# Scores ahead of the transposes in a fused cross attention and mixture-of-experts kernel, with keys stored apart and read in 64-float runs

## The chip, the cores and the metric

The kernel runs on one core of a Trainium2 chip. The time is that of the device for one execution, in microseconds; the lower the better. Three executions of the kernel before were timed, and one was profiled.

## What is computed

128 independent batches of 128 tokens with 256 channels go through an attention block and a feed-forward block. Attention is across the 16 heads of one token, not across tokens: for each token a 16 x 16 matrix of scores. Cut to what matters:

```python
q = (layernorm(x) @ Wq.T).reshape(B, N, H, D)      # H = D = 16
k = (ctx @ Wk.T).reshape(B, N, H, D)
v = (ctx @ Wv.T).reshape(B, N, H, D)
attn = softmax(einsum('bnhd,bngd->bnhg', q, k) * SCALE, axis=-1)
x = x + transpose(einsum('bnhg,bngd->bnhd', attn, v), (0, 2, 1, 3)).reshape(B, N, C) @ Wp.T + bp
n = layernorm(x)
shared = (silu(n @ sfc1.T) * (n @ sfc2.T)) @ sfc3.T
top_w, top_idx = top_k(n @ gate_w.T, 2); top_w = softmax(top_w)
moe = sum over the two chosen experts e of top_w * (silu(n @ w1[e].T) @ w2[e].T)
out = x + moe + shared
```

## The kernel before

The work has two stages. In the first a loop goes over 32 chunks of four batches (512 tokens, four tiles of 128). Body c of the loop mixes three chunks: the attention of chunk c, the shared feed-forward and the routing of chunk c-1, and the projections of chunk c+1. The routed rows are scattered to lists in DRAM. In the second stage the lists are read back by expert, four tiles at a time, and go through the experts' matrices; the change does not touch it.

Every engine has its own program, written out by hand in the order in which it runs, and waits on counting semaphores. For the change these parts matter:

- **TensorE**, body c: `scores(c)` (128 matmuls, L1202, of blocks of q, `q_rows`, with blocks of keys, `k_diag`) into the banks A0 and A1; `gate(c-1)` (L1211) from the transposed rows `xn2_t` (printed as th) into A2; `project(c+1)`: four tiles of keys and values in the banks U, A0, Y0, Y1 (L1187 to L1189, three matmuls for each half of the channels, since operands are split in a high and a low part), then two pairs of q tiles in A1 and U; then the shared feed-forward of c-1 in steps z and u, with `attend(c)` (L1345) and `attend_out(c)` (L1361, L1366) in between; `shared_down(c-1)` (48 matmuls into Y0 and Y1, out of wsh_out and hid_hi, hid_lo); last `turn(c)`, eight transposes (L1387) of the normalised rows xn into Z0 and Z1.
- **ScalarE**, body c: the exponentials of the probabilities (L564) and of the routing (L598, needs VectorE's routing, which needs the gate); `project_out(c+1)`: four copies of keys and values from PSUM (L582), one store of 1 MB (L584), four scaled copies of q (L590), a store of 512 KB (L593); then `load_res(c)`, the load of the residual rows (L633, behind a wait on base_ready); tanh and rounding of the shared part; the normalisation (L647, four instructions); `turned_out(c)`: two copies of the transposed rows to th (L653), rounding of the next x (L573), rounding of th (L658).
- **SP**, chunk c: loads of the next x and ctx, then, when the scores of c-1 are done, eight reads of keys (L277), eight of q (L282), and, when the attention of c-1 is done, eight of values (L290). They turn the layout round: from token on the partition, as stored, to head channel (keys, q) or head (values) on the partition. All 24 read 64 KB each in runs of 16 floats, 1024 runs each.
- **GpSimd**, body c: the low parts of th (xn_lo), base scatters (L421), half of the scaling of the probabilities (L450), eight slot scatters (L412) and four low parts of the hidden rows (L443, hid_lo) by turns; small powers; then the low parts of ctx and x for c+2 (L426, ctx_lo and hid_lo). `shared_down` waits for three of the four hid_lo at its start and for the fourth after 18 matmuls.
- **VectorE**, body c: row maxima (L790) and shift (L784) of the scores, routing, sums, transposes of the probabilities, products of the shared part, `bias_add(c)` on the residual rows (L922), attention's low parts (L917), the residual sums (L931, which count h2_ready) and moments.

`w_sb` stands for several tensors in the printed names, among them `w2_sb`, which holds the keys and values on their way to DRAM and `q_rows`. hid_hi and hid_lo hold x's parts too.

## Time and profile before

| | us |
|---|---|
| three timed runs | 1759.50, 1761.28, 1775.06 |
| median | 1761.28 |
| profiled execution, as timed | 1761.56 |
| its span in the profile | 1759.7 |

| engine | busy us | share | instructions |
|---|---|---|---|
| PE (TensorE matmul) | 1510.9 | 86% | 17237 |
| PEld (TensorE weight load) | 1321.4 | 75% | 17238 |
| DVE (VectorE) | 1279.3 | 73% | 3352 |
| ACT (ScalarE) | 747.6 | 42% | 1442 |
| POOL (GpSimd) | 1308.6 | 74% | 1252 |

How to read the rows further down. A row of the timeline has the start in us, the duration, the engine, the line of the kernel, the operation, what it writes and reads, shapes, the number of instructions merged in it, and in brackets the engine's idle time before it with what ended it. SPq and ACTq are the queues' issues of DMAs; such a row's duration is the time in which they were issued, not the transfer. A row of the waits has: engine and line, what it waited for, us in total, times, the longest in us. A row of sums by window has: the window, its length, then for PE, PEld, DVE, ACT and POOL the busy us with the number of instructions in brackets, then the granted clock of TensorE as a share of full speed (2.4 GHz; 0.5 is the lower level of 1.2 GHz), the busy share of the DMA engines, and GB/s. Starts and ends of matmuls overlap, since they are pipelined.

### The profile page before, as it was taken

Reading aid. Unit: us, or ns where it says so; the run is one execution under the profiler, and the core shown is the slowest. Engines: PE = TensorE matmul, PEld = TensorE weight load, DVE = VectorE, ACT = ScalarE, POOL = GpSimd, SP = SyncE. Lnnn points to the kernel's source line nnn. Section 1 sums busy time; section 2 is a strip of 40 time slices with the busy share of each in tenths; the row PEclk is TensorE's granted clock in tenths of the full one; section 3 lists DMA queues with packets and bytes.
Section 4 is the critical chain, followed back from the end, with each engine's and each line's share of the span. In section 5 each row is a group of like instructions: output and inputs, shape, how many; then the busy total and the mean of one; then the engine's idle time right before and its main releaser. Section 6 shows DMA issues by size and latency. Waiting matters only on the chain.

```text
span 1759.7 us, 50976 instructions
## 1 busy us (share of the span) xinstructions
PE 1510.9 (86%) x17237; PEld 1321.4 (75%) x17238; DVE 1279.3 (73%) x3352; ACT 747.6 (42%) x1442; POOL 1308.6 (74%) x1252
## 2 busy tenths in 40 slices
PE   5599999999999999999999999987577677777774
PEld 4488888888888888888888888875577676676764
DVE  7578888788888878887888886886455655555553
ACT  3344455444554455454554454533133333332331
POOL 4277787777788777887787877776587777677776
PEclk9799999999999999999999999998798988888987
DMA  8788888888888887898888888873778777677773
GB/s 221 125 198 194 178 176 188 209 188 185 165 207 207 179 176 165 225 195 172 175 172 236 182 180 164 179 189 116 243 232 241 232 236 220 178 234 229 225 222 109
DMA packets 945836, 340.80 MB, mean 194 GB/s; under 512 B 824571, under 2 KB 899213, under 8 KB 940771
## 3 DMA queue, kind: packets, MB, share of 16 engines
q1 hardware_dynamic: 892464, 166.19, 53.3%
q0 software_dynamic: 33600, 88.95, 13.6%
q10 hardware_dynamic: 19728, 85.13, 12.8%
q8 instruction: 21, 0.34, 0.1%
q14 instruction: 23, 0.18, 0.0%
HBM read 200.37 MB, written 148.15 MB: 198 GB/s over the span
## 4 chain that ended last, share of the span: by engine, by line
SPq 26%; issue 22%; PE 17%; DMA 12%; POOL 8%; DVE 7%; another core or an unknown queue 4%; ACT 3%; DVEq 1%; POOLq 0%; ACTq 0%
SPq L277 10%; SPq L282 9%; DMA kv_dram<-w_sb 5%; SPq L290 5%; DMA w_sb<-q_dram 4%; POOL sums L529 3%; PE bank_a L1202 3%; POOL out L529 2%; PE bank_y L1187 2%; POOL xn_lo L521 2%; PE bank_y L1189 2%; DMA h<-in_x_res 2%; PE bank_y L1188 2%; PE bank_z L1473 2%
## 5 line engine op out<-in xcount | busy, mean ns | idle before, releaser
L412 POOL DMA_INDIRECT slots<-xn,slot_i x256 | 277.5, 1084 | 86.0 <-issue 71.4
L1142 DVE SCALAR_TENSOR_TENSOR v_area<-bank_y,tail,v_area 128x256 f32<-128x256 f32 x288 | 121.9, 478 | 129.9 <-PE bank_y L1189 65.5
L1187 PE MATMUL bank_y<-w_hi,xn_hi 128*128 x288 | 100.7, 350 | 110.7 <-POOL xn_lo L521 94.5
L529 POOL DMA_INDIRECT out<-v_area,tail x144 | 147.1, 1021 | 57.2 <-issue 34.4
L529 POOL DMA_INDIRECT sums<-v_area,tail x144 | 147.9, 1027 | 43.8 <-issue 35.9
L729 ACT ACTIVATE th<-bank_z 128x512 f32<-128x512 f32 x72 | 43.0, 598 | 285.1 <-PE bank_z L1473 151.1
L1187 PEld LDWEIGHTS bank_y<-w_hi,xn_hi 128*128 128x128 f32 x288 | 60.0, 208 | 128.4 <-issue 128.1
L421 POOL DMA_INDIRECT sums<-k_area,slot_i x128 | 126.7, 990 | 35.8 <-issue 30.1
L1187 PE MATMUL bank_y<-wsh_out_hi,hid_hi 128*128 128x256 f32 x512 | 142.1, 278 | 0.0
L1189 PE MATMUL bank_y<-wsh_out_hi,hid_lo 128*128 128x256 f32 x512 | 142.1, 278 | 0.0
L1188 PE MATMUL bank_y<-wsh_out_lo,hid_hi 128*128 128x256 f32 x512 | 142.0, 277 | 0.0
L614 ACT ACTIVATE th<-bank_z 128x512 f32<-128x512 f32 x128 | 76.2, 596 | 114.9 <-PE bank_z L1189 56.4
L1120 DVE SCALAR_TENSOR_TENSOR v_area<-th,bank_z 128x512 f32<-128x512 f32 x72 | 49.3, 684 | 96.9 <-ACT th L729 48.9
L790 DVE TENSOR_REDUCE row_max<-bank_a 128x32 f32<-128x512 f32 x64 | 44.3, 692 | 91.8 <-PE bank_a L1202 91.8
L647 ACT ACTIVATE xn<-h,ln_shift,ln_rstd 128x256 f32<-128x256 f32 x128 | 66.6, 592 | 101.2 <-POOL ln_shift L402 98.2
L619 ACT ACTIVATE hid_hi<-k_area 128x512 fp32r<-128x512 f32 x64 | 40.5, 632 | 162.6 <-DVE k_area L900 102.9
L1187 PE MATMUL bank_z<-xn_hi,w_lo 128*128 128x512 f32 x256 | 105.0, 410 | 5.0 <-DVE th L890 2.7
L443 POOL TENSOR_TENSOR hid_lo<-k_area,hid_hi 128x512 fp32r<-128x512 f32 x64 | 83.0, 1296 | 28.0 <-ACT hid_hi L619 27.2
L1189 PE MATMUL bank_z<-xn_hi,w_lo 128*128 128x512 f32 x256 | 101.7, 397 | 0.0
L1188 PE MATMUL bank_z<-xn_lo,w_lo 128*128 128x512 f32 x256 | 101.2, 395 | 0.0
L1473 PE MATMUL bank_z<-k_area,x_sb 128*128 128x128 f32 x576 | 89.3, 320 | 12.3 <-ACT k_area L722 11.0
L722 ACT ACTIVATE k_area<-bank_a 128x512 f32<-128x512 f32 x144 | 80.6, 597 | 45.0 <-issue 19.9
(234 smaller groups left out, 5314.2 us busy)
## 6 DMA issues: line engine op xcount, KB each, us to landing
k_area<-slots SPq DMA_DIRECT2D x288, 129.0 KB
v_area<-sums SPq DMA_DIRECT2D x288, 128.0 KB
kv_dram<-w_sb ACTq DMA_DIRECT2D x32, 1024.0 KB
x_sb<-in_x_in SPq DMA_DIRECT2D x32, 512.0 KB
ctx_sb<-in_ctx_t SPq DMA_DIRECT2D x32, 512.0 KB
q_dram<-q_sb ACTq DMA_DIRECT2D x32, 512.0 KB
k_area<-kv_dram SPq DMA_DIRECT2D x256, 64.0 KB
w_sb<-q_dram SPq DMA_DIRECT2D x256, 64.0 KB
```

The source lines that it names most:

```text
L277: sp.dma_start(k_diag[rows, :, t % 4, :], kv[src, :, :, 0, :].rearrange("n i (d g) -> d (n i) g", d=D)).then_inc(S["qk_read"], 16)
L282: sp.dma_start(q_rows[rows, :, t // 4 * H:(t // 4 + 1) * H], q[src].rearrange("n i (d h) -> d (n i) h", d=D)).then_inc(S["qk_read"], 16)
L290: sp.dma_start(v_diag[16 * r:16 * r + 16, :, r % 4, :], kv_t2[t2, :, i, 1, :].rearrange("m (g d) -> g m d", g=H)).then_inc(S["v_read"], 16)
L412: pool.indirect_dma_start(slots[j], bass.IndirectOffsetOnAxis(ap=slot_i[:, par, j, i:i + 1], axis=0), row_of[j][:, i, :], None).then_inc(S ...
L421: pool.indirect_dma_start(sums[FIRST], bass.IndirectOffsetOnAxis(ap=slot_i[:, par, FIRST, i:i + 1], axis=0), base[:, i, :], None).then_inc ...
L443: nc.gpsimd.tensor_tensor(hid_lo[:, s, :], hid_of[s], hid_hi[:, s, :], ALU.subtract).then_inc(S["hid_split"], 1)
L529: pool.indirect_dma_start(target, bass.IndirectOffsetOnAxis(ap=tail[:, r, t, 1 - j:2 - j].bitcast(u32), axis=0), y_ring[:, r, t, :], None, ...
L1142: st = nc.vector.scalar_tensor_tensor(out=y_ring[:, r, t, :], in0=Y[t // 2][:, t % 2 * C:(t % 2 + 1) * C], scalar=tail[:, r, t, j:j + 1], ...
L1187: mm(out, lhs_hi, rhs_hi, start=start, stop=False)
L1188: mm(out, lhs_hi, rhs_lo, start=False, stop=False)
L1189: return mm(out, lhs_lo, rhs_hi, start=False, stop=stop)
L1473: last = mm(Z[r % 2][:, t * P:(t + 1) * P], w1_slot[r % 2][:, t, k * HID:(k + 1) * HID], x_ring_t[:, t, k * P:(k + 1) * P], start=k == 0, ...
```

## The change

Three things are changed in the chunk loop.

- Keys and values go to DRAM apart, `k_dram` and `v_dram`, by two stores of 512 KB: keys, then q, then values. ScalarE's copy writes the keys in the order channel of the head, tile, head, so that for one channel the 16 heads of all four tiles are 64 floats in a row, and `k_diag` takes them in that order. A key read has 256 runs of 64 floats. Reads of q and of values keep 16 floats.
- TensorE computes `scores(c)` ahead of `turn(c-1)`, with a wait for the residual sums of c-1, whose banks the scores take, and `gate(c-1)` stands behind the first tile of keys and values of `project(c+1)`.
- ScalarE issues the load of the residual ahead of `project_out`.

```diff
-                kv = kv_dram[c].rearrange("(t n) (i w f) -> t n i w f", t=8, i=BPC, w=2)
+                k = k_dram[c].rearrange("(t n) (d i g) -> t d n (i g)", t=8, d=D, i=BPC)
...
-                    sp.dma_start(k_diag[rows, :, t % 4, :],
-                                 kv[src, :, :, 0, :].rearrange("n i (d g) -> d (n i) g", d=D)).then_inc(S["qk_read"], 16)
+                    sp.dma_start(k_diag[rows, :, t % 4, :, :].rearrange("p n i g -> p n (i g)"), k[src]).then_inc(S["qk_read"], 16)
...
-                    nc.scalar.activation(kv_sb[:, i, :], KV_BANKS[i][:, :], ACT.Copy).then_inc(S["kv_out"], 1)
+                    nc.scalar.activation(kv_by_tile[:, i], KV_BANKS[i][:, :].rearrange("p (w x y) -> p w x y", w=2, x=D), ACT.Copy).then_inc(S["kv_out"], 1)
                 act.wait_ge(S["kv_out"], at(4, c, 4))
-                act.dma_start(kv_dram[c], kv_sb).then_inc(S["kv_stored"], 16)
+                act.dma_start(k_dram[c], k_sb).then_inc(S["k_stored"], 16)
...
                 act.dma_start(q_dram[c], q_sb[:, :, :]).then_inc(S["q_stored"], 16)
+                act.dma_start(v_dram[c], v_sb).then_inc(S["v_stored"], 16)
...
-                if ahead:
-                    project_out(c + 1, False)
                 if first:
                     act.wait_ge(S["w_ffn_split"], 2)
                 else:
                     act.wait_ge(S["base_ready"], at(2, c - 1, 0))
                 load_res(c, par)
+                if ahead:
+                    project_out(c + 1, False)
...
                 pe.wait_ge(S["qk_read"], at(256, c, 256))
+                if not first:
+                    pe.wait_ge(S["h2_ready"], at(2, c, 0))
...
                             last = mm(SCORE_BANKS[u][32 * a:32 * a + 32, n * 4 * H:(n + 1) * 4 * H], q_rows[:, m, :],
-                                      k_diag[:, m, :, :].rearrange("p t g -> p (t g)"), start=True, stop=True)
+                                      k_diag[:, u * 8 + n, :, QUARTER_OF[a], :], start=True, stop=True)
...
                     last.then_inc(S["kv_full"], 1)
+                    if gate_of is not None and i == 0:
+                        gate(gate_of)
...
             def body(c, first, ahead):
                 scores(c, False)
-                gate(c - 1)
+                turn(c - 1)
                 if ahead:
-                    project(c + 1, False, True, first)
+                    project(c + 1, False, True, first, c - 1)
+                else:
+                    gate(c - 1)
...
                 shared_down(c - 1, first)
-                turn(c)
```

On TensorE, at the start of body 1, before (ident and xn are the transposes, k_area with w_sb the scores, wgate_sb the gate, w_hi with ctx_hi the keys and values):

```order
L1387 MATMUL bank_z<-ident,xn 128x128 [waits const_ready,xn2_ready,const_in,w_ffn]
L1387 MATMUL bank_z<-ident,xn 128x128 [waits xn2_ready] x3
L1387 MATMUL bank_z<-ident,xn 128x128 x4
L1202 MATMUL bank_a<-k_area,w_sb 32x64 [waits qk_read]
L1202 MATMUL bank_a<-k_area,w_sb 32x64 x63
L1211 MATMUL bank_a<-th,wgate_sb 32x128 [waits t2_out]
L1211 MATMUL bank_a<-th,wgate_sb 32x128 x7
L1187 MATMUL bank_u<-w_hi,ctx_hi 128x512 [waits ctx_split]
L1188 MATMUL bank_u<-w_hi,ctx_hi 128x512
L1189 MATMUL bank_u<-w_hi,ctx_lo 128x512
```

And there after the change (lines are those of the changed kernel):

```order
L1209 MATMUL bank_a<-k_area,w_sb 32x64 [waits qk_read,const_ready,h2_ready,const_in,w_ffn]
L1209 MATMUL bank_a<-k_area,w_sb 32x64 x63
L1396 MATMUL bank_z<-ident,xn 128x128 [waits xn2_ready] x4
L1396 MATMUL bank_z<-ident,xn 128x128 x4
L1192 MATMUL bank_u<-w_hi,ctx_hi 128x512 [waits ctx_split]
L1193 MATMUL bank_u<-w_hi,ctx_hi 128x512
L1194 MATMUL bank_u<-w_hi,ctx_lo 128x512
L1192 MATMUL bank_u<-w_hi,ctx_hi 128x512
L1193 MATMUL bank_u<-w_hi,ctx_hi 128x512
L1194 MATMUL bank_u<-w_hi,ctx_lo 128x512
L1218 MATMUL bank_a<-th,wgate_sb 32x128 [waits t2_out]
L1218 MATMUL bank_a<-th,wgate_sb 32x128 x7
```

The scores moved from behind the transposes to ahead of them, with the wait for h2_ready, and the gate from ahead of the first tile in bank U to behind it.

On ScalarE, in a body behind the loop that still projects ahead, before:

```order
L598 ACTIVATE gap_e<-top 128x1 x3
L582 ACTIVATE w_sb<-bank_u 128x512 [waits kv_full,q_stored,kv_stored]
L582 ACTIVATE w_sb<-bank_a 128x512 [waits kv_full]
L582 ACTIVATE w_sb<-bank_y 128x512 [waits kv_full] x2
L584 DMA kv_dram<-w_sb 128x2048 [waits kv_out]
L590 ACTIVATE q_sb<-bank_a,ln_rstd 128x256 [waits q_full,ln1_pow]
L590 ACTIVATE q_sb<-bank_a,ln_rstd 128x256
L590 ACTIVATE q_sb<-bank_u,ln_rstd 128x256 [waits q_full]
L590 ACTIVATE q_sb<-bank_u,ln_rstd 128x256
L593 DMA q_dram<-q_sb 128x1024 [waits q_out]
L633 DMA h<-in_x_res 128x1024 [waits base_ready]
```

And after:

```order
L603 ACTIVATE gap_e<-top 128x1 x3
L638 DMA h<-in_x_res 128x1024 [waits base_ready]
L586 ACTIVATE w_sb<-bank_u 128x32x16 [waits q_stored,kv_full,v_stored,k_stored]
L586 ACTIVATE w_sb<-bank_a 128x32x16 [waits kv_full]
L586 ACTIVATE w_sb<-bank_y 128x32x16 [waits kv_full] x2
L588 DMA k_dram<-w_sb 128x1024 [waits kv_out]
L594 ACTIVATE q_sb<-bank_a,ln_rstd 128x256 [waits q_full,ln1_pow]
L594 ACTIVATE q_sb<-bank_a,ln_rstd 128x256
L594 ACTIVATE q_sb<-bank_u,ln_rstd 128x256 [waits q_full]
L594 ACTIVATE q_sb<-bank_u,ln_rstd 128x256
L597 DMA q_dram<-q_sb 128x1024 [waits q_out]
L598 DMA v_dram<-w_sb 128x1024
```

The residual's load moved from the end to the head of these rows, the one store became two, and the values' store stands behind q's.

## Rows read from the trace of the kernel before

**Rows 1.** Sums by window: the middle of the loop, and 804 to 808 us.
```profile
400.00:800.00 400.00, 387.04 (x5058) 332.12 (x5057) 337.89 (x875) 200.47 (x397) 317.36 (x278) 1.00 0.86 189
804.00:808.00 4.00, 3.69 (x140) 3.69 (x144) 0.76 (x2) 1.49 (x3) 3.47 (x2) 0.57 0.58 57
```
**Rows 2.** Instructions of line 790, 150 to 1170 us: min/median/max ns, first and last start.
```profile
L790 DVE TENSOR_REDUCE row_max<-bank_a x58: 691/692/693, 154.4 to 1169.4; 128x32 f32<-128x512 f32 x58
```
**Rows 3.** Timeline of PE, the head of the chunk at 547.5 us.
```profile
547.52 0.54 PE L1387 MATMUL bank_z<-ident,xn 128*128 128x128 f32 x2
...
548.71 0.77 PE L1387 MATMUL bank_z<-ident,xn 128*128 128x128 f32 x5 [0.16 <-ACT xn L647]
549.67 1.99 PE L1202 MATMUL bank_a<-k_area,w_sb 128*32 128x64 f32 x128 [0.20 <-DMA w_sb<-q_dram]
551.49 0.66 PE L1211 MATMUL bank_a<-th,wgate_sb 128*32 128x128 f32 x16
552.07 0.50 PE L1187 MATMUL bank_u<-w_hi,ctx_hi 128*128 128x512 f32 x1
```
**Rows 4.** Waits, 150 to 1170 us.
```profile
DVE h L922 <- DMA h<-in_x_res: 20.6, 22, 2.2
PEld bank_a L1202 <- DMA w_sb<-q_dram: 14.7, 18, 2.9
```
**Rows 5.** Timeline of PE, the scores of the three longest waits.
```profile
333.38 3.60 PE L1202 MATMUL bank_a<-k_area,w_sb 128*32 128x64 f32 x128 [1.17 <-DMA w_sb<-q_dram]
...
804.31 3.57 PE L1202 MATMUL bank_a<-k_area,w_sb 128*32 128x64 f32 x128 [1.57 <-DMA w_sb<-q_dram]
...
1058.56 3.64 PE L1202 MATMUL bank_a<-k_area,w_sb 128*32 128x64 f32 x128 [2.66 <-DMA w_sb<-q_dram]
```
**Rows 6.** Timeline of SP's queue, the chunk behind the one of rows 3.
```profile
555.26 0.51 SPq L263 DMA_DIRECT2D x_sb<-in_x_in  x1
...
565.69 7.53 SPq L277 DMA_DIRECT2D k_area<-kv_dram  x8
573.40 7.89 SPq L282 DMA_DIRECT2D w_sb<-q_dram  x8
```
**Rows 7.** Timeline of PE: first matmul of the down projection, first transposes behind it.
```profile
578.04 0.28 PE L1187 MATMUL bank_y<-wsh_out_hi,hid_hi 128*128 128x256 f32 x1
...
583.49 0.53 PE L1387 MATMUL bank_z<-ident,xn 128*128 128x128 f32 x2
```
**Rows 8.** Timeline of POOL, from the context's low part to the last hidden part.
```profile
548.10 2.36 POOL L426 TENSOR_TENSOR ctx_lo<-ctx_sb,ctx_hi 128x1024 fp32r<-128x1024 f32 x1
551.27 2.39 POOL L426 TENSOR_TENSOR hid_lo<-hid,hid_hi 128x1024 fp32r<-128x1024 f32 x1 [0.81 <-ACT hid_hi L573]
...
576.60 0.96 POOL L412 DMA_INDIRECT slots<-xn,slot_i  x1 [0.30 <-issue]
578.20 1.30 POOL L443 TENSOR_TENSOR hid_lo<-k_area,hid_hi 128x512 fp32r<-128x512 f32 x1 [0.64 <-ACT hid_hi L619]
```
**Rows 9.** Timeline of ACT, the copies of the transposed rows.
```profile
549.07 1.08 ACT L653 ACTIVATE th<-bank_z 128x512 f32<-128x512 f32 x2 [0.42 <-PE bank_z L1387]
```
**Rows 10.** Timeline: bias addition in two chunks; first transposes behind the second.
```profile
534.07 1.23 DVE L922 TENSOR_TENSOR h<-h,bias_sb 128x1024 f32<-128x1024 f32 x1 [1.36 <-DMA h<-in_x_res]
...
605.54 2.96 DVE L922 TENSOR_TENSOR h<-h,bias_sb 128x1024 f32<-128x1024 f32 x1 [1.32 <-DMA h<-in_x_res]
...
620.41 0.53 PE L1387 MATMUL bank_z<-ident,xn 128*128 128x128 f32 x2
```
**Rows 11.** Timeline of SP's queue and of PE in the first 80 us.
```profile
27.54 5.54 SPq L277 DMA_DIRECT2D k_area<-kv_dram  x8
...
59.44 3.64 PE L1345 MATMUL bank_a<-v_area,w_sb 128*32 128x64 f32 x128 [10.29 <-DMA v_area<-kv_dram]
...
72.48 2.71 PE L1387 MATMUL bank_z<-ident,xn 128*128 128x128 f32 x8 [4.90 <-ACT xn L647]
...
76.47 3.64 PE L1202 MATMUL bank_a<-k_area,w_sb 128*32 128x64 f32 x128 [1.28 <-DMA w_sb<-q_dram]
```

## What the change will do to the time

> **What bounds the kernel now.** I read the sums by window first. Between 400 and 800 us, in the middle of the chunk loop, TensorE is busy 387 of 400 us at the full clock, VectorE 338, GpSimd 317 [rows 1]. The loop is bound by TensorE, and there is little idle time to win. The row maxima of the scores, two a chunk, run from 154.4 to 1169.4 us in 58 instances [rows 2]: 28 chunks and some 0.9 us, so a chunk takes (1015 - 0.9) / 28 = 36.2 us. The expert stage behind the loop is not touched by the change, and I leave it as it is.
>
> The busy share hides short waits, so next I read the timeline of TensorE around the head of one ordinary chunk [rows 3]. I call D the moment at which the down projection has issued its last matmul, here 547.52. The transposes (L1387) start at once but come in pieces, two, one and five, because each waits for ScalarE's normalised rows. Scores (L1202) start at 549.67 after 0.20 us of waiting for q's rows to land, the gate (L1211) at 551.49, the first tile of keys and values at 552.07, D + 4.55. The scores themselves need 1.82 us, the gate 0.58, eight transposes without waits about 8 x 0.11 = 0.9 (five take 0.77 with the 0.33 tail of one). That is 3.3 of the 4.55 us; the rest is the wait for the rows and for the DMA.
>
> Then who else is nearly late. The waits of the stretch say that the scores waited for q's rows 18 times in 29 chunks, 14.7 us by the weight loads, and that VectorE's bias addition (L922) waited 20.6 us 22 times for the residual's load [rows 4]. The longest of the first kind cost more than the wait: in three chunks TensorE idled 1.17, 1.57 and 2.66 us, and the 128 score matmuls that followed took 3.60, 3.57 and 3.64 us in place of 1.99 [rows 5]. The stretch at 804 us was granted 0.57 of the clock, mostly the 1.2 GHz level, where the loop else has 1.00 [rows 1]: after a longer pause the engine ran at the lower level.
>
> **The change, step by step.** *Layout of the keys.* A key read moves the same 64 KB in 256 runs of 64 floats, not 1024 of 16. Eight reads keep SP for 7.53 us, the eight of q for 7.89 behind them, until 581.29, 2.2 us ahead of this chunk's end at D = 583.49 [rows 6, 7]; landing takes about that, since the scores of the chunk before waited 0.20 us for q's rows and started at D + 2.15 [rows 3]. Nothing in this trace has 256-byte runs of this kind. If only bytes counted, eight reads would stay at 7.5 us, if only runs counted 1.9. I take 4.0, nearer to the runs, since the stores and loads with long runs hold their queues for far less per byte (an input of 512 KB takes SP 0.51 us, all eight key reads together move that much) [rows 6]. So q's rows land about 3.5 us sooner, near D - 1.4. For the new order to work they must come at least 2.15 us sooner, so 1.35 us are to spare. The Trainium skill, DMA: Bandwidth & Descriptors, section "Why small descriptors are slow (HBM only)", gives a fixed 3 cycles a packet beside one per 32 bytes: 5 cycles for 64 bytes, 11 for 256. By that estimate eight reads would take 7.53 x 11 / (4 x 5) = 4.1 us; no run here shows it yet.
>
> *Two stores.* 512 KB of keys go first, then q, then the values. Bytes are unchanged, keys can only be readable sooner. I count nothing for it: the values are read by a queue that reaches them after key and q reads, after 7.53 and 7.89 us of other reads [rows 6], and ScalarE's one more issue (SP's of an input takes 0.51) falls where it waits for TensorE anyway. The copies of keys and values write 16-float pieces, and the scores read them with a stride; ScalarE's and TensorE's durations should not change, and if the copies took half as long again, four of them would be 1.2 us a chunk on an engine that is busy 200 of 400 us [rows 1].
>
> *Order on TensorE.* From D: scores 1.82; the rows are normalised by then, so the transposes run through, 0.9, to D + 2.7. The first tile of keys needs GpSimd's low part of the context, which ends at 548.10 + 2.36 = D + 2.94 [rows 8]: start at D + 3.0. The gate behind it costs its 0.58. The second tile therefore stands where it would stand with a first tile at D + 3.58: 4.55 - 3.58 = 0.97 us sooner. The added wait for the residual sums is over by then (they precede the normalised rows). The second tile's bank waits for VectorE's shifted scores; they have the transposes, the first tile and the gate as cover, where before they had the gate and the tile. The gate ends at D + 5.0, before at D + 4.55. Behind it wait VectorE's routing, then ScalarE's four gap exponentials, and behind those on ScalarE the key and value copies (L582) and so kv_out, which TensorE needs for attention and shared banks; ScalarE comes to them only after the probabilities' exponentials, which the transposes' copies move back anyway.
>
> *What is late next.* ScalarE's copies of the transposed rows (L653) start at 549.07, D + 1.55 [rows 9]; with the scores ahead they start at D + 1.82 + 0.44 + 0.3 = D + 2.56, one microsecond later, and all that follows them: the rounding of x, then GpSimd's hid_lo at 551.27 [rows 8]. From there GpSimd has a long fixed list (two splits, four base scatters, the scaling of the probabilities, eight slot scatters, three hidden splits) until 576.60 + 0.96 = 577.56, that is 26.29 us. Then comes the fourth hidden split, which in this chunk waited 0.64 us for ScalarE and took 1.30 [rows 8]. TensorE asks for it 18 matmuls (two tiles, three quarters, three each) after the start of the down projection, whose 48 take 583.49 - 578.04 = 5.45 us: 578.04 + 18 x 0.1135 = D + 32.56 [rows 7]. Before: done at 579.50, D + 31.98, in time. After: D + 4.75 + 26.29 + 0.15 + 1.30 = D + 32.49, wanted at D + 31.59. GpSimd would be 0.9 us late, and give back nearly all of the 0.97. So a chunk gains between 0.06 us (the list as long as here) and 0.97 (the list never late). The list holds instructions stretched by other engines (below), and in other chunks is shorter; I take 0.4.
>
> *The residual's load* is issued ahead of ScalarE's eight copies and the stores, not behind them. That ends L922's waits [rows 4]. Such a wait cost a chunk time where it pushed the addition into GpSimd's scatters: 1.23 us at 534.07, but 2.96 at 605.54 after 1.32 us of waiting, and that chunk lasted from 583.49 to 620.41, 36.9 us, against 36.0 for the one before [rows 7, 10]. I credit 0.1 us a chunk.
>
> *Start.* The first chunks are a chain of reads on SP: key reads of 5.54 us from 27.54, then TensorE waits 10.29 us for the values until 59.44, then 4.90 for normalised rows, then 1.28 for q's rows, and the scores run 3.64 us at the low clock [rows 11]. Shorter key reads bring all this forward by about 2 us, and the second set of them lets scores stand inside the 4.90 us wait: 1.28 + 3.64. Together 7 us, between 4 (half of the second part) and 10.
>
> **Sum.** 28 chunks x 0.5 = 14.0; the three long chunks lose their excess, (1.17 - 0.20) + (3.60 - 1.99) = 2.6, then 3.0 and 4.1, 9.7 together; start 7. That is 30.7 us of the profiled span, 1759.7 to 1729. The median of the runs, 1761.28, lies 1.6 above that span (the profiled execution itself was timed at 1761.56), so the time is 1731 us.
>
> **The rivals.** *TensorE keeps everything* (20%). GpSimd's list turns out shorter by 0.9 us, because fewer of its instructions meet VectorE's. For it: its busy share is 317 of 400. Then 28 x 0.97 = 27, with 9.7 and 10: 1714.
>
> *GpSimd takes the loop* (17%). The list stays at 26.3 us, a chunk gains under 0.1: 1761.3 - 9.7 - 7 - 1.7 = 1743. For it: the list above, worked out for a chunk of ordinary length.
>
> *Reads still late* (6%). Eight key reads keep more than 5.3 us, or q's store is not there. Scores then wait with the transposes behind them, first tile at D + 2.1 + 1.82 + 0.9 = 4.8: no gain in a chunk, the long ones stay; 4 us of the start: 1757.
>
> *Slower, through the port of VectorE and GpSimd* (8%). The bias addition no longer waits and GpSimd is 1 us later, so the two meet at another place. If the addition takes 2.96 us in every chunk, each lasts 36.9 in place of 36.2: 28 x 0.7 = 20 us more, less the 7 of the start: 1774. It decides once a mean chunk is 0.25 us longer than now. Against it: most chunks meet somewhere already. The Trainium skill, SBUF — State Buffer, section "SBUF: two separate sides", says that a VectorE operation with two SBUF inputs and a GpSimd operation that reads SBUF exclude each other for a whole instruction; the two durations of L922 agree with that.
>
> The remaining 4% are for what I don't see. My own case (45%) has 1722 to 1742.
>
> **Chances.** About 1% is what a measurement of this kernel can tell from no change: 17.6 us, a limit of 1743.7. Faster by more: my case, the first rival and half of the second, 0.73. Slower by more (over 1779) only with a part of the last: 0.04. The range goes from the first rival's 1714, a little widened, to what is left when GpSimd takes the loop and the long chunks stay: 1761 - 7 - 2 = 1752.
>
> **What would show it.** Right: scores directly behind the down projection with no wait for q's rows, transposes in one piece, key reads at about 4 us for eight, no stretch of low clock in the loop, L922 without waits, and new waits of the down projection (L1187, bank_y) for GpSimd's hid_lo of up to 0.9 us. A chunk near 35.4 us with these. Wrong: no such waits and a chunk of 34.9; key reads near 7 us; or the waits of the down projection above 1 us. The expert stage has to take the same time.

## The result, and the profile after

Over twenty runs of each kernel on one chip the changed kernel takes 1754.6 us (median, 1745.19 to 1768.6), the kernel before 1766.92 us (1757.25 to 1776.45). The ratio is 0.9934, with a 95% interval of 0.9913 to 0.9955: faster by two thirds of a percent, which is inside the 1% that I called no change. I had forecast 1731 us, a ratio of 0.983 to the 1761.28 us known then, and a range of 1712 to 1752 us. The result lies outside that range on the slow side. Part of this is the kernel before, which took 5.6 us more over twenty runs than over the three known then; the ratio times 1761.28 is 1749.7 us, just inside the range. The profiled execution has a span of 1752.3 us, against 1759.7 before.

The first view is the same as in [rows 1] and [rows 2]: busy time by window and the row maxima of the scores (L795, L790 before), for the changed kernel. The last row is that of the kernel before, with one more chunk at its start than in [rows 2].

```profile
400.00:800.00 400.00, 387.11 (x5052) 331.50 (x5045) 310.07 (x876) 200.82 (x407) 321.32 (x277) 1.00 0.82 189
804.00:808.00 4.00, 4.00 (x22) 3.38 (x21) 3.41 (x6) 0.97 (x3) 3.25 (x4) 1.00 0.63 190
L795 DVE TENSOR_REDUCE row_max<-bank_a x60: 690/692/693, 108.4 to 1152.7; 128x32 f32<-128x512 f32 x60
```
```profile
L790 DVE TENSOR_REDUCE row_max<-bank_a x60: 691/692/693, 114.8 to 1169.4; 128x32 f32<-128x512 f32 x60
```

TensorE is as busy as before. The maxima of the third chunk come 6.4 us sooner (108.4 against 114.8), those of the last 16.7 us sooner: 6.4 us were won at the start and 10.3 in 29 chunks. A chunk takes (1152.7 - 108.4 - 0.9) / 29 = 35.98 us, against 36.33 worked out in the same way, where I expected 35.4. The sum credited the three long chunks with 9.7 us, and they are gone; so the ordinary chunks won 0.6 us together (10.3 less 9.7), where the sum had 14. Measured from D to D, the chunks with the full clock took 35.92 us in the mean before (24 of 27) and take 36.01 us now (27 of 27). The span shrank by only 7.4 us; the other 9.3 went in the expert stage, which the change doesn't touch. The profiled executions of this study differ by tens of microseconds there, so I compare chunks by profiles and whole kernels by ratios.

The head of a chunk, attention and the chunk's neighbours, in the changed kernel. Timelines: start, duration, engine, line; in brackets the idle time ahead and what ended it.

```profile
575.50 1.99 PE L1209 MATMUL bank_a<-k_area,w_sb 128*32 128x64 f32 x128
577.42 1.09 PE L1396 MATMUL bank_z<-ident,xn 128*128 128x128 f32 x8
578.44 0.50 PE L1192 MATMUL bank_u<-w_hi,ctx_hi 128*128 128x512 f32 x1
...
596.43 0.65 PE L1354 MATMUL bank_a<-v_area,w_sb 128*32 128x64 f32 x31
597.43 1.27 PE L1354 MATMUL bank_a<-v_area,w_sb 128*32 128x64 f32 x66 [0.36 <-issue]
599.17 0.33 PE L1354 MATMUL bank_a<-v_area,w_sb 128*32 128x64 f32 x3 [0.47 <-issue]
599.89 0.67 PE L1354 MATMUL bank_a<-v_area,w_sb 128*32 128x64 f32 x28 [0.40 <-issue]
600.49 0.50 PE L1192 MATMUL bank_z<-xn_hi,w_lo 128*128 128x512 f32 x1
```
```profile
580.31 2.41 POOL L429 TENSOR_TENSOR hid_lo<-hid,hid_hi 128x1024 fp32r<-128x1024 f32 x1 [1.93 <-ACT hid_hi L576]
...
595.36 1.54 POOL L415 DMA_INDIRECT slots<-xn,slot_i  x1 [0.30 <-issue]
596.93 1.28 POOL L446 TENSOR_TENSOR hid_lo<-hid,hid_hi 128x512 fp32r<-128x512 f32 x1
598.38 0.99 POOL L415 DMA_INDIRECT slots<-xn,slot_i  x1 [0.17 <-issue]
...
606.39 1.30 POOL L446 TENSOR_TENSOR hid_lo<-k_area,hid_hi 128x512 fp32r<-128x512 f32 x1 [0.55 <-ACT hid_hi L624]
```
```profile
588.63 4.85 SPq L279 DMA_DIRECT2D k_area<-k_dram  x8
...
594.85 1.22 DVE L927 TENSOR_TENSOR h<-h,bias_sb 128x1024 f32<-128x1024 f32 x1
```

The head is what I had drawn: with D, the end of the down projection's issue as in the prediction, at 575.41, scores at D + 0.09 with no wait, eight transposes in one piece, the first tile of keys at D + 3.03. L927 (L922 before) no longer waits, and no stretch of the loop runs at the low clock. What I hadn't drawn is the attention, the 128 matmul rows of L1354: from 596.43 to 600.49 they take 4.06 us and stop three times, for 0.36, 0.47 and 0.40 us, with no semaphore behind it ("issue"). The waits of the loop say how often. First the changed kernel, 150 to 1170 us, then the kernel before, 150 to 1150 us: engine, tile, line, what was waited for; us in total, times, longest.

```profile
PEld bank_a L1354 <- issue: 54.4, 113, 1.3
PE bank_a L1354 <- issue: 30.4, 84, 0.5
```
```profile
PEld bank_a L1345 <- issue: 20.3, 55, 0.7
PE bank_a L1345 <- issue: 5.3, 20, 0.5
```

So what the head won was gone before the chunk's end: the median attention grew from 2.4 to 3.8 us (first matmul of it to the next section's first). Where it doesn't stop it takes 1.9. The question for the experiments was what stops it, and whether that sets the chunk's length.

### The profile page after: what moved, and what is told of

Its sections match the earlier page's. It is cut to its first block, busy times and chain, and to the rows that moved or that the text cites. A ratio compares the mean times of both kernels' runs of the same rounds, so it can differ in the third digit from the quotient of the medians.

```text
span 1752.3 us, 50714 instructions
## 1 busy us (share of the span) xinstructions
PE 1506.9 (86%) x17237; PEld 1323.2 (76%) x17238; DVE 1214.8 (69%) x3352; ACT 740.1 (42%) x1442; POOL 1310.0 (75%) x1252
## 3 DMA queue, kind: packets, MB, share of 16 engines
q1 hardware_dynamic: 695856, 166.19, 48.9%
## 4 chain that ended last, share of the span: by engine, by line
PE 65%; issue 15%; POOL 6%; another core or an unknown queue 5%; DVE 3%; SPq 3%; ACT 1%; DMA 1%; DVEq 0%; POOLq 0%; ACTq 0%
PE bank_y L1194 7%; PE bank_y L1192 7%; PE bank_y L1193 7%; PE bank_a L1354 5%; PE bank_z L1192 4%; PE bank_a L1209 3%; PE bank_z L1194 3%; PE bank_z L1193 3%; PE bank_a L1192 3%; POOL out L532 3%; PE bank_u L1192 3%; PE bank_u L1194 2%; PE bank_u L1193 2%; PE bank_a L1194 2%
## 5 line engine op out<-in xcount | busy, mean ns | idle before, releaser
L429 POOL TENSOR_TENSOR hid_lo<-hid,hid_hi 128x1024 fp32r<-128x1024 f32 x32 | 78.1, 2439 | 65.0 <-ACT hid_hi L576 65.0
L1354 PE MATMUL bank_a<-v_area,w_sb 128*32 128x64 f32 x4096 | 90.2, 223 | 41.8 <-issue 30.8
L1354 PEld LDWEIGHTS bank_a<-v_area,w_sb 128*32 128x32 f32 x4096 | 70.7, 111 | 67.6 <-issue 56.4
L1483 PE MATMUL bank_z<-k_area,ctx_sb 128*128 128x128 f32 x576 | 91.9, 326 | 31.5 <-ACT k_area L727 28.7
L895 DVE SCALAR_TENSOR_TENSOR th<-th,bank_z 128x512 f32<-128x512 f32 x128 | 87.5, 683 | 36.7 <-issue 30.6
L1483 PEld LDWEIGHTS bank_z<-k_area,ctx_sb 128*128 128x128 f32 x576 | 86.7, 238 | 34.6 <-ACT k_area L727 25.1
L1192 PE MATMUL bank_z<-xn_hi,w_lo 128*128 128x512 f32 x256 | 105.1, 410 | 5.5 <-POOL xn_lo L429 2.8
L812 DVE STREAM_TRANSPOSE w_sb<-w_sb 64x512 f32<-64x512 f32 x128 | 90.4, 706 | 17.3 <-POOL w_sb L453 14.1
```

Of the source, the lines that this page charges most:

```text
L429: nc.gpsimd.tensor_tensor(lo, value[:, :, :], hi, ALU.subtract).then_inc(S[done], 1)
L812: nc.vector.transpose(turned_half(u, f), prob[rows, u, :].rearrange("p (s h) -> p s h", h=H)).then_inc(S["p_ready"], 1)
L895: nc.vector.scalar_tensor_tensor(out=th[:, s % 2, :], in0=th[:, s % 2, :], scalar=1.0, in1=Z[s % 2][:, :], op0=ALU.add, op1=ALU.mult).then ...
L1192: mm(out, lhs_hi, rhs_hi, start=start, stop=False)
L1354: last = mm(O_BANKS[u][32 * pair:32 * pair + 32, n * 4 * D:(n + 1) * 4 * D], prob_t[:, 32 * g:32 * g + 32], v_diag[:, pair * 16 + u * 8 + ...
L1483: last = mm(Z[r % 2][:, t * P:(t + 1) * P], w1_slot[r % 2][:, t, k * HID:(k + 1) * HID], x_ring_t[:, t, k * P:(k + 1) * P], start=k == 0, ...
```

## The experiments

Eighteen runs were made in five sets, of thirteen edited kernels (e1 to e13) and five repeats (c1 to c5); those that share a chip and a median of the kernel before in the table were timed beside the same runs of it. The letters stand for four chips; whether the first chip is one of them isn't on record. On chip B the kernel before itself moved from 1776.41 to 1755.99 us between two sets, so ratios are compared inside a set, and what compares chips is weaker. "Attention" is the median of the loop's chunks, measured as above; a chunk is worked out from the row maxima, as for the result.

| run | chip | kernel before, us | ratio [95%] | chunk, us | attention, us |
|---|---|---|---|---|---|
| result | first | 1766.92 | 0.9934 [0.9913, 0.9955] | 36.0 | 3.8 |
| e1, PE loop written out | A | 1776.5 | 0.9999 [0.9974, 1.0023] | 36.1 | 3.8 |
| e2, V store later | A | 1776.5 | 1.0016 [0.9990, 1.0043] | 36.1 | 3.9 |
| e3, delay at the head | A | 1776.5 | 1.0186 [1.0165, 1.0206] | 36.9 | 3.9 |
| e4, code shifted | A | 1776.5 | 1.0008 [0.9984, 1.0031] | 36.0 | 3.9 |
| c1, changed again | B | 1776.41 | 0.9985 [0.9965, 1.0006] | 36.0 | 3.9 |
| e5, scatters off the attention | B | 1776.41 | 1.0008 [0.9984, 1.0032] | 35.8 | 1.9 |
| e6, no q reads | B | 1776.41 | 1.0012 [0.9988, 1.0036] | 35.8 | 3.8 |
| e7, layout only | B | 1776.41 | 0.9876 [0.9830, 0.9922] | 35.3 | 2.5 |
| e8, x rounded first | B | 1755.99 | 0.9792 [0.9740, 0.9844] | 34.9 | 2.4 |
| e9, e8 and last scatter late | B | 1755.99 | 1.0059 [1.0033, 1.0085] | 36.1 | 1.9 |
| e10, e7 and last scatter late | B | 1755.99 | 1.0526 [1.0460, 1.0591] | 38.7 | 1.9 |
| e11, order only | B | 1755.99 | 1.0243 [1.0179, 1.0307] | 37.3 | 3.7 |
| e12, e8 and five scatters first | C | 1698.38 | 1.0266 [1.0241, 1.0291] | 37.2 | 1.9 |
| e13, residual load only | C | 1698.38 | 0.9986 [0.9970, 1.0003] | 35.6 | 1.9 |
| c2, e8 again | C | 1698.38 | 0.9862 [0.9840, 0.9885] | 34.9 | 1.95 |
| c3, changed a third time | D | 1708.14 | 0.9813 [0.9787, 0.9838] | 35.0 | 1.94 |
| c4, layout only again | D | 1708.14 | 0.9853 [0.9826, 0.9880] | 35.2 | 1.97 |
| c5, e8 a third time | D | 1708.14 | 0.9802 [0.9777, 0.9827] | 34.9 | 1.95 |

### Set 1: is it the code, the traffic, or the supply?

e1 replaces TensorE's loop by straight code:

```diff
-            with pe.Fori(2, CHUNKS - 1) as c:
+            for c in range(2, CHUNKS - 1):
                 body(c, False, True)
```

> The changed kernel with TensorE's loop over chunks 2 to 30 written out 29 times, nothing else. In the changed kernel the attention matmuls (128 rows of 32x64) take 3.8 us in a loop chunk, with pauses of 0.6 us in which no semaphore is waited for, and 1.8 us in the chunks 1 and 31 that stand outside the loop. Theory L (the pauses belong to the hardware loop: its jump, or where its body lies in memory): the attention takes 1.8 to 2.0 us in every chunk, a chunk 34 to 35 us, the whole 1715 to 1730 us. Theory D (the transfers in flight at that moment hold TensorE's instructions up): nothing changes, attention 3.8 us, the whole within 5 us of the changed kernel's 1754.6. Theory S (TensorE's sequencer can supply only so many instructions per chunk, whatever the code looks like): nothing changes either.

e2 issues the store of V later on ScalarE:

```diff
                 act.dma_start(q_dram[c], q_sb[:, :, :]).then_inc(S["q_stored"], 16)
-                act.dma_start(v_dram[c], v_sb).then_inc(S["v_stored"], 16)
...
                 o_round(sums_of)
+                act.dma_start(v_dram[c + 2], v_sb).then_inc(S["v_stored"], 16)
```

> The changed kernel, but the store of V (1 MB less a half: 128x1024 floats) leaves ScalarE's queue only after the attention output has been rounded, some 5 us after the attention matmuls, so that it isn't in flight beside them. Theory D (transfers in flight hold up TensorE's instructions): the attention drops from 3.8 us towards 1.9 to 2.4 us and a chunk from 36.0 towards 35 us, the whole towards 1725 us. Theories L and S: attention stays at 3.8 us, the whole within 5 us of 1754.6; it may get longer where V's reads come late.

e3 and e4 add matmuls, the one in every chunk, the other once, ahead of everything:

```diff
                 scores(c, False)
+                for i in range(4):
+                    mm(KV_BANKS[0][:, :], wsh_hi[:, 0, 0:P], wsh_hi[:, 0, 0:BANK], start=True, stop=True)
                 turn(c - 1)
```

> The changed kernel with four extra f32r matmuls of 128x512 (about 0.23 us each, 0.9 us together) between the scores and the transposes of every chunk but the first. Their result is overwritten. Theory S (the supply of instructions sets the pace; what TensorE saves at the head it waits in the attention): the attention gets shorter by nearly the same 0.9 us, a chunk stays within 0.2 us of 35.99, the whole within 6 us of 1754.6. Theories L and D: attention stays at 3.8 us, a chunk takes 0.9 us more, the whole is 1780 us.

```diff
                     pe.wait_ge(S["ones_ready"], 1)
+                    for i in range(32):
+                        mm(WQ_SUM_BANK[0:32, 0:64], ones_f[:, 0:32], ones_f[:, 0:64], start=True, stop=True)
```

> The changed kernel with 32 extra small fp32 matmuls (32x64) in TensorE's program ahead of the first projection, where TensorE waits for its weights anyway (under 2 us once, hidden or not). Inside the loop every instruction is the same, but stands further on in memory. Theory L in the form that the place of the body in memory decides where the supply pauses: the pauses of 0.6 us move to another place of the chunk (by about 64 to 128 rows), and the attention's 3.8 us change; a chunk may take 34.5 to 36.5 us. Theories D and S, and L in the form that the jump itself costs the time: the pauses stay at the attention's rows 28 to 31 and 107 to 125, the whole within 5 us of 1754.6.

None of the four moved the attention by more than 0.1 us. (The changed kernel itself was not run on chip A; the four are held against it by chunk and attention, not by ratio.) e1 is the cleanest, since the DMA view counts the fetched code; its row for queue q8 (packets, MB, share), which rises with TensorE's written-out program, in the changed kernel and in e1:

```profile
q8 instruction: 21, 0.34, 0.1%
```
```profile
q8 instruction: 122, 2.00, 0.5%
```

With the loop written out 101 more blocks are fetched, and the pauses are the same, the first most often after 29 or 30 of the 128 matmuls in both kernels: neither the jump nor the fetching of code makes them. e4 added 32 matmuls ahead of the loop and left the pauses in place (the first after 27 to 30 in 23 of 28 chunks). e3's added 1.04 us came out as 0.9 us more a chunk with the attention unchanged, so TensorE is not held by a fixed supply per chunk either. e2 left the first pause and brought the second forward, from 2.74 to 2.29 us behind the attention's start in the median, and GpSimd's second scatter issue of that stretch moved alike, from 2.14 to 1.68. That was the hint: the pauses keep their distance to GpSimd's indirect DMA issues, not to TensorE's own code.

### Set 2: GpSimd's scatters, q's reads, and the change in parts

> The changed kernel as it is, run beside the others so that they are compared on one chip. Every theory: 0.993 of the kernel before, attention 3.8 us in a loop chunk, a chunk 36.0 us.

```diff
-                scatter(c - 1, 1 - par, SCATTERS[:4])
-                hid_split(c - 1, range(1))
-                scatter(c - 1, 1 - par, SCATTERS[4:5])
-                hid_split(c - 1, range(1, 2))
-                scatter(c - 1, 1 - par, SCATTERS[5:6])
+                scatter(c - 1, 1 - par, SCATTERS[:3])
+                hid_split(c - 1, range(2))
+                scatter(c - 1, 1 - par, SCATTERS[3:5])
                 hid_split(c - 1, range(2, 3))
-                scatter(c - 1, 1 - par, SCATTERS[6:])
+                scatter(c - 1, 1 - par, SCATTERS[5:])
```

> The changed kernel with GpSimd's list in another order: three slot scatters, both first hid_lo subtractions, two scatters, the third subtraction, three scatters, the last subtraction (as it is: four scatters, subtraction, scatter, subtraction, scatter, subtraction, two scatters, subtraction). Same instructions, but none of GpSimd's indirect DMA issues (1.0 to 1.7 us each; in the changed kernel one from 1.0 us ahead of the attention to 0.7 us into it, the next from 2.15 to 3.1 us into it) falls into the attention matmuls. Theory P (while GpSimd issues an indirect DMA, TensorE's sequencer gets its instructions late, which shows only where TensorE runs its shortest instructions): attention falls from 3.8 to 1.9 to 2.2 us, a chunk from 36.0 to 34.2 to 34.8 us, the whole by 35 to 50 us against the changed kernel of this call. Theory Q (the reads of q's rows in 64-byte pieces, in flight through the attention, hold it up): attention stays at 3.5 to 3.9 us, the whole within 5 us.

In e6 SP's loop over the eight reads of q runs in the first chunk alone, and TensorE waits for 128 instead of 256 a chunk.

> The changed kernel without the eight reads of q's rows from the second chunk on: scores are made from the rows of chunk 0, so their values aren't the reference's; every matmul and everything else still runs. Theory Q (these reads hold TensorE up in the attention): attention 1.9 to 2.2 us, a chunk 34.5 us. Theory P (GpSimd's indirect DMA issues do): attention stays at 3.4 to 3.9 us and a chunk within 0.4 us of 36.0; the pauses keep their place beside GpSimd's issues.

e7 takes the changed kernel and puts TensorE's body back:

```diff
                 scores(c, False)
-                turn(c - 1)
+                gate(c - 1)
                 if ahead:
-                    project(c + 1, False, True, first, c - 1)
+                    project(c + 1, False, True, first)
...
                 shared_down(c - 1, first)
+                turn(c)
```

> The changed kernel with TensorE's order of before (transposes at the end of the chunk, gate behind the scores), so only the layout of keys, the two stores and the residual load's new place are left of the change. By my prediction's sum the layout alone should give nothing in an ordinary chunk (the head is 6.45 us either way) and take away the long chunks and some of the start: 0.990 to 0.997 of before. Theory P: the attention matmuls stand where they stood against GpSimd's list, so they take 2.2 to 2.8 us, not 3.8, and the kernel is as fast as the changed one or faster: the order's gain is what the pauses take back. Theory Q: the reads of q's rows again overlap the attention by their earlier start, so attention is 3 us or more.

e6 fells theory Q: with no q reads in flight the attention still takes 3.8 us. e5 agrees with theory P. Its attention and GpSimd beside it:

```profile
630.61 2.21 PE L1352 MATMUL bank_a<-v_area,w_sb 128*32 128x64 f32 x128
```
```profile
628.42 0.96 POOL L415 DMA_INDIRECT slots<-xn,slot_i  x1 [0.30 <-issue]
629.41 1.30 POOL L446 TENSOR_TENSOR hid_lo<-hid,hid_hi 128x512 fp32r<-128x512 f32 x1
631.59 1.36 POOL L446 TENSOR_TENSOR hid_lo<-hid,hid_hi 128x512 fp32r<-128x512 f32 x1 [0.88 <-ACT hid_hi L622]
633.11 0.98 POOL L415 DMA_INDIRECT slots<-xn,slot_i  x1 [0.16 <-issue]
```

One piece, 1.92 us up to the next section (the row's 2.21 holds the tail of the last matmul), with a subtraction of GpSimd beside it and no issue: what goes with the pauses is the indirect DMA issue, not GpSimd's work as such. The reverse stands in e10 (below), inside one kernel: in 8 of its 26 attentions between 150 and 1150 us two issues fall into the attention, which takes 3.75 to 4.47 us; in the other 18 none does, and it takes 1.92 to 1.94. One of the eight:

```profile
674.07 1.76 PE L1351 MATMUL bank_a<-v_area,w_sb 128*32 128x64 f32 x108
675.98 0.27 PE L1351 MATMUL bank_a<-v_area,w_sb 128*32 128x64 f32 x3 [0.15 <-issue]
676.70 0.32 PE L1351 MATMUL bank_a<-v_area,w_sb 128*32 128x64 f32 x4 [0.44 <-issue]
677.45 0.32 PE L1351 MATMUL bank_a<-v_area,w_sb 128*32 128x64 f32 x4 [0.44 <-issue]
```
```profile
675.42 0.99 POOL L415 DMA_INDIRECT slots<-xn,slot_i  x1 [0.15 <-issue]
676.71 0.96 POOL L415 DMA_INDIRECT slots<-xn,slot_i  x1 [0.30 <-issue]
```

But the second half of my expectation failed: a chunk of e5 takes 35.8 us, not 34.2 to 34.8. The down projection (48 matmuls, 5.53 us without waits) now takes 6.39, since hid_lo(3), GpSimd's fourth and last low part of the hidden rows, ends at D + 32.2. Part of that is e5's own order: the second subtraction, at 631.59, now waits 0.88 us for ScalarE. So e5 shows that the pauses go with the issues, and not what a chunk would take without pauses and with the list as it was. e7 was a surprise the other way: the layout without the order, expected at 0.990 to 0.997, is 0.988, a chunk of 35.3 us, with its attention at 2.5 us as theory P had it.

### Set 3: GpSimd's start

In the changed kernel ScalarE rounds x behind the copies of the transposed rows, and these now come later. e8 turns the two around:

```diff
             def turned_out(c, ahead_2, early=False):
+                if ahead_2 and early:
+                    act.wait_ge(S["acc_full"], at(2, c - 1, 2))
+                    x_round(c + 2)
                 for k in range(KT):
                     act.wait_ge(S["t2_full"], at(KT, c, k + 1))
                     nc.scalar.activation(xn2_t[:, k, :], XN2T_BANKS[k][:, :], ACT.Copy).then_inc(S["t2_out"], 1)
-                if ahead_2:
+                if ahead_2 and not early:
                     x_round(c + 2)
```

> The changed kernel with one step of ScalarE moved: the rounding of x for the chunk after next (x_hi) stands ahead of the copies of the transposed rows instead of behind them, behind a wait for the down projection. In the changed kernel these copies wait for the transposes, which now come 2.0 us later in the chunk, so x_hi is ready 4.83 us after the down projection (D) instead of 3.68, and GpSimd's x subtraction starts at D+4.91 instead of D+3.76; its list then runs to hid_lo(3) at D+32.2, nearly without a stop. Theory G (the loop of the changed kernel is held by GpSimd's list, which starts 1.15 us later: any pause in the attention that goes away only comes back as a wait for hid_lo(3), as the quiet order showed: attention 1.92 us, down projection 6.39 instead of 5.53, chunk 35.7): here the subtraction starts at about D+3.0, so a chunk falls to what TensorE takes with pauses, 34.5 to 35.5 us, the whole to 0.97 to 0.988 of before. Without theory G (TensorE's pauses alone set the changed kernel's 35.99): a chunk within 0.3 us of 36.0.

e9 and e10 add to e8 and to e7 one order of GpSimd's list: scatters [:4], two subtractions, [4:6], the third, [6:7], the fourth, [7:]. e11 is the kernel before with TensorE's new body alone.

> As the run before it, and GpSimd's list in an order that keeps its indirect DMA issues out of the attention matmuls: four scatters, two hid_lo subtractions, two scatters, the third subtraction, a scatter, the fourth subtraction, the last scatter. If both halves hold (GpSimd's list starts early enough, and its issues cause TensorE's pauses): attention 1.9 us, no wait for hid_lo(3) (down projection 5.5 us), a chunk 33.9 to 34.5 us, the whole 0.96 to 0.975 of before. If only GpSimd's start mattered: the same as the run before it.

> The layout-only kernel (TensorE's order of before; 0.988 of before, a chunk 35.1 us, attention 2.5 us) with the same order of GpSimd's list as in the run before it. Theory P: attention 1.92 us in every loop chunk, a chunk 34.4 to 34.8 us, unless GpSimd's wait for hid_hi(1) makes its list too late (then down projection over 5.6 us and a chunk 35 us); the whole 0.97 to 0.985 of before.

> The kernel before with only TensorE's new order (scores, transposes, keys of tile 0, gate, the rest); layout, stores and the place of the residual load as before. By my prediction's sum the order alone wins 0.97 us at the head less 0.5 given back: a chunk 35.9 us. Theory G: GpSimd's x subtraction starts at D+4.9 here too and the chunk is bound at 35.7 to 36.0 us; the reads of keys and queries, still in pieces of 64 bytes, must be done 1.9 us earlier against D than before, so the scores wait for them in most chunks: a chunk 36 to 36.6 us, the whole 1.00 to 1.01 of before.

e8 is the fastest version: 0.979 of before. Its timeline, with D at 594.61:

```profile
594.70 1.99 PE L1212 MATMUL bank_a<-k_area,w_sb 128*32 128x64 f32 x128
...
615.66 2.43 PE L1357 MATMUL bank_a<-v_area,w_sb 128*32 128x64 f32 x128
```
```profile
597.52 2.41 POOL L429 TENSOR_TENSOR hid_lo<-hid,hid_hi 128x1024 fp32r<-128x1024 f32 x1
...
615.63 1.79 POOL L415 DMA_INDIRECT slots<-xn,slot_i  x1 [0.16 <-issue]
...
624.55 1.29 POOL L446 TENSOR_TENSOR hid_lo<-k_area,hid_hi 128x512 fp32r<-128x512 f32 x1 [0.64 <-ACT hid_hi L624]
```

The subtraction of x (hid_lo, 128x1024) starts at D + 2.91 instead of D + 4.90, and hid_lo(3) at the end of the list waits for ScalarE and no one waits for it. The list's earlier start also moved it against the attention, where now one issue falls instead of two, and 2.37 us are left. So e8 changes two things at once, the list's end and the pauses; set 5 says more on which of them counts.

e9 kept the attention at 1.92 us, e10 in 18 chunks of 26, and both lost more elsewhere. The waits of e9, 150 to 1100 us (e10 has 126.6 us in 25 chunks on the same row):

```profile
ACT xn L651 <- DMA slots<-xn,slot_i: 142.2, 26, 6.1
```

A scatter reads the rows of xn2 that ScalarE overwrites next. Behind the last subtraction it lands so late that normalisation ends at D + 3.5 (e9) where it ended at D + 1.14. In e10, where the scores stand behind the transposes, TensorE waits longer with it, and 10 of its 25 chunks hold a stretch at the clock's 1.2 GHz level besides. That is my own edit's fault and says nothing against theory P. e11, expected at 1.00 to 1.01, is 1.024: the old layout's reads come too late for the early scores, and the residual's load, which e11 leaves at its old place, comes too late for the bias. Its waits, 150 to 1100 us:

```profile
DVE h L922 <- DMA h<-in_x_res: 59.1, 21, 3.5
...
PE bank_a L1204 <- DMA w_sb<-q_dram: 11.8, 10, 1.7
```

### Set 4 and 5: what was open, on chips without pauses

e12 is e8 with GpSimd's list as scatters [:5], two subtractions, [5:7], one, [7:], one. e13 is the kernel before with load_res ahead of project_out on ScalarE.

> The kernel with x rounded first (e8: a chunk 34.9 us, attention 2.37 us with one pause beside the scatter that GpSimd issues at the attention's start, 0.979 of before) with GpSimd's list as five scatters, two subtractions, two scatters, one subtraction, one scatter, the last subtraction. All scatters still stand ahead of hid_lo(3), so the rows of xn2 come free as early as before (in the earlier quiet order the last scatter stood behind it, and the normalisation waited for it until D+3.5 instead of D+1.14). Theory P: no indirect issue falls into the attention, which takes 1.92 us, and unless hid_lo(3) is late (it ends at D+31.0 and is needed at D+31.7) a chunk takes 34.4 to 34.6 us and the whole 0.965 to 0.977 of before. Against it: a pause that stays in the attention with no indirect issue beside it, or a down projection over 5.7 us.

> The kernel before with one edit of the change alone: ScalarE issues the residual load ahead of the projections' copies instead of behind them. The layout-only kernel (0.988 of before) holds this edit, the keys' layout and the two stores. My prediction gave this edit 0.1 us a chunk, so 0.998 to 1.000. If it is this edit that makes the ordinary chunk of the layout-only kernel 0.8 us shorter than before's, this run takes 0.98 to 0.99 of before and DVE's addition of the bias (L922) no longer waits; if it is the keys' layout, it stays at 0.997 to 1.003.

> The kernel with x rounded first again, beside the run with the scatters early, so that the two are compared on one chip: 0.974 to 0.985 of before, a chunk 34.9 us, attention 2.37 us.

This set brought something that no theory had: on chip C no kernel pauses in the attention, e8 (c2) and e13 included, although GpSimd's issues stand beside it as before. The attention of c2, with GpSimd's and VectorE's rows beside it, can be laid next to e8's rows above, which have the same kernel at the same time of the span:

```profile
615.62 2.05 PE L1357 MATMUL bank_a<-v_area,w_sb 128*32 128x64 f32 x128
```
```profile
615.64 1.78 POOL L415 DMA_INDIRECT slots<-xn,slot_i  x1 [0.16 <-issue]
```
```profile
614.75 1.81 DVE L930 TENSOR_TENSOR h<-h,bias_sb 128x1024 f32<-128x1024 f32 x1
```

The issue takes 1.78 us here and 1.79 in e8, so its length is not what parts the chips. It goes with VectorE: between 150 and 1150 us all 29 slot scatters of c2 that take over 1.3 us have the bias addition beside them.

e13, at 0.9986 [0.997, 1.0003], bounds the residual's load: 0 to 0.3% on this chip, my 0.1 us a chunk being 0.2%. So e7's 1.2% comes in the main from the keys' layout, with the two stores that it brings.

e12 failed: expected at 0.965 to 0.977, it is 1.027. It kept the issues off the attention, but a chunk takes 37.2 us. VectorE's bias addition, the groups of 150 to 1100 us (total and mean ns behind the first bar), in e12 and then in c2; below them, for e12, TensorE's longest wait, the addition with GpSimd's rows beside it, and the sum of a window behind such a wait:

```profile
L928 DVE TENSOR_TENSOR h<-h,bias_sb 128x1024 f32<-128x1024 f32 x26 | 107.4, 4131 | 0.0
```
```profile
L930 DVE TENSOR_TENSOR h<-h,bias_sb 128x1024 f32<-128x1024 f32 x27 | 49.9, 1849 | 0.0
```
```profile
PEld bank_a L1371 <- ACT ctx_hi L641: 48.9, 26, 2.0
```
```profile
644.80 2.53 POOL L446 TENSOR_TENSOR hid_lo<-hid,hid_hi 128x512 fp32r<-128x512 f32 x2
...
644.41 4.00 DVE L928 TENSOR_TENSOR h<-h,bias_sb 128x1024 f32<-128x1024 f32 x1
```
```profile
653.00:657.00 4.00, 3.94 (x20) 3.94 (x21) 2.95 (x7) 0.79 (x2) 1.54 (x2) 0.57 1.19 123
```

The addition takes 4.13 us in the mean, where it takes 1.85 in c2 and 1.22 in the changed kernel: two subtractions of GpSimd, back to back, now stand inside it. What waits behind it on VectorE reaches the attention's projection over hid_hi and ctx_hi, 48.9 us in 26 chunks. Behind that wait the granted clock mostly fell, as in the window of 653 us, 0.57: of 26 chunks measured from D to D, 19 hold some 3.4 us at the 1.2 GHz level and last 37.5 to 37.9 us, the other seven 35.9 to 36.4. So of the 2.3 us a chunk that e12 lost to c2 (37.2 against 34.9), about 1.0 is the low clock behind the wait. This is my rival of the port between VectorE and GpSimd, in another kernel. By the Trainium skill, SBUF — State Buffer, section "SBUF: two separate sides", a VectorE operation with two SBUF inputs and a GpSimd operation that reads SBUF exclude each other for a whole instruction; the trace agrees with that in the sum, since 1.22 us alone and 2.53 us of two subtractions make 3.75 of the 4.00.

> The changed kernel, a third time. On the chip of the last three runs TensorE showed no pause in the attention (1.95 us with a scatter of GpSimd issued right beside it), on the chips before it did. If GpSimd's list is what holds the changed kernel (theory G: x's subtraction starts at D+4.9, hid_lo(3) ends 27.2 us later, the rest of the down projection and the way to D take 3.5 us): a chunk takes 35.6 to 36.0 us whether the attention takes 3.8 us or 1.9, and where it takes 1.9, the attention's projection or the down projection waits for the difference. If TensorE's pauses hold it: 36.0 us with pauses, 34.2 to 34.6 us without.

> The layout-only kernel beside the changed one and the one with x rounded first, on one chip: 0.983 to 0.993 of before, faster than the changed kernel by 0.5 to 1.2%. A chunk 35.2 to 35.4 us.

> The kernel with x rounded first, on the same chip as the changed and the layout-only kernel: 0.975 to 0.988 of before, the fastest of the three by 0.2 to 1%. A chunk 34.9 us, as on both chips before, with the attention at 2.4 us or at 1.95.

Chip D has no pauses either. c3, the unchanged edit, is there 0.981 of before. TensorE, GpSimd, and the waits of 150 to 1170 us:

```profile
615.53 1.99 PE L1354 MATMUL bank_a<-v_area,w_sb 128*32 128x64 f32 x128
...
626.09 0.39 PE L1192 MATMUL bank_y<-wsh_out_hi,hid_hi 128*128 128x256 f32 x1 [0.82 <-POOL hid_lo L446]
```
```profile
614.63 1.12 POOL L415 DMA_INDIRECT slots<-xn,slot_i  x1 [0.30 <-issue]
...
624.76 1.28 POOL L446 TENSOR_TENSOR hid_lo<-k_area,hid_hi 128x512 fp32r<-128x512 f32 x1
```
```profile
PEld bank_y L1192 <- POOL hid_lo L446: 25.1, 28, 1.0
```

Here is the wait that the prediction forecast, in every one of 28 chunks, up to 1.0 us. My expectation for c3 held one half and missed the other: the difference is waited for at the down projection, as theory G says, but a chunk takes 34.96 us, below its 35.6. GpSimd's list ends sooner here, hid_lo(3) at D + 31.3 in the median instead of D + 32.0. The fourth scatter's issue ahead of the attention takes 1.12 us, where it takes 1.54 in the changed kernel's first trace. Since e8 and c2 have issues of one length with and without pauses, I read nothing out of that.

The two other expectations of this set failed. The layout alone (c4) was to beat the changed kernel by 0.5 to 1.2% and is 0.4% behind it. And e8 (c5) was to be the fastest by 0.2 to 1%: it is 0.9802 [0.9777, 0.9827] against the changed kernel's 0.9813 [0.9787, 0.9838], with a chunk of 34.9 us against 34.96, which is no difference. In c5 the wait for hid_lo is gone, and TensorE waits for VectorE at the attention's projection instead (150 to 1100 us):

```profile
PEld bank_a L1378 <- DVE ctx_lo L925: 19.9, 27, 1.1
```

So rounding x first, worth 1.1 us a chunk on chip B (34.9 against 36.0), is worth nothing where TensorE doesn't pause. That speaks for the pauses, and against the end of GpSimd's list, as what e8 repaired on B; it is a comparison between chips.

## Why the prediction was wrong, point by point

**The head.** Right: scores at D + 0.09, transposes in one piece, first tile at D + 3.0, as drawn. Eight key reads keep SP for 4.85 us in the chunk shown, where I took 4.0, and 4.2 to 5.6 in the loop; it was enough, no scores wait.

**The long chunks and the start.** Right. No low clock in the loop, and 6.4 us at the start where I had 7.

**The residual's load.** Right: L927 waits for nothing, and e13 puts the edit at 0.997 to 1.000 of before, which holds my 0.1 us. The addition itself became shorter too, 1.22 us in every chunk where it took 1.65 in the mean.

**What is late next.** The mechanism is there, but not in the result that was to be forecast: on the chips with pauses TensorE comes late itself, and the down projection hardly waits (0.3 us once in c1's loop). The sign that I gave for it (down projection waiting for hid_lo, up to 0.9 us) is there in c3, 1.0 us at the longest. With x rounded first the wait is gone, but on chip D no time with it (c5). The size was a little pessimistic: hid_lo(3) ends at D + 32.0 in the result's trace and at D + 31.3 in c3, where I had 32.49, and c3's chunk is 34.96 us where I had 35.4. That c3's ratio, 0.9813, is close to my 0.983 is in part luck, since the kernel before is faster on that chip too.

**The step that failed** is in the term 28 x 0.5, of which the ordinary chunks paid next to nothing (35.92 us before, 36.01 after): I took the rest of the chunk, attention included, to cost TensorE what it cost before, and costed GpSimd's shift only by when its list *ends*. In its place the attention took 1.4 us more. What the shift does in the *middle* of the list was not looked at. In the chunk shown, GpSimd's fourth slot scatter starts 1.1 us ahead of the attention and reaches into it, and the fifth follows 1.95 us behind its start; in the same chunk of the kernel before, the fourth was over. Two indirect DMA issues fall into it instead of one. On chips where that matters, the attention takes 3.8 us instead of 2.4, more than the head's 0.97. The kernel before had the sign: 55 pauses of "issue" in its attention, 20.3 us by the weight loads, that I hadn't listed. Comparing chunks of c1 or the result (36.0) with c3 (34.96), the changed kernel takes 1.0 us a chunk more on the chips with pauses, 29 us or 1.7% of the time. But the kernel before takes more there as well, 36.2 us [rows 2] against 35.6 in e13, which is that kernel but for the residual's load. So some 0.4 us of the gain of a chunk are lost on those chips, 12 us or 0.7%; the ratios, 0.9934 and 0.9985 against 0.9813, differ by 1.2% and 1.7%, and the rest is not explained. Whole sets on other chips are compared there, so it is an estimate and not a removal of the cause alone; e5, which is one, exchanged the pauses for GpSimd's lateness.

**The share of each part** I also had wrong. The layout alone is 0.988 [0.983, 0.992] and 0.985 [0.983, 0.988] on two chips, where I had 0.990 to 0.997. One reason is that it ends the scores' waits for q's rows in ordinary chunks too (they start at D + 1.9 instead of D + 2.1 in the median); I had counted these under the order. In chunks with the full clock, from D to D, it gives 35.3 us on chip B against 35.9 of the kernel before on the first chip, but 35.2 on chip D against 35.3 of e13 on chip C; why so much less there is not shown. On top of the layout the order costs 0.7 us a chunk on chip B (36.0 against 35.3) and wins 0.3 on chip D (34.96 against 35.2). Without the layout it makes the kernel slower (e11, though with the old place of the residual's load).

**Rivals.** "Reads still late", at 1757 us, came nearest by its number, and that is chance: no scores waited and the long chunks went. "GpSimd takes the loop", at 1743, had an ordinary chunk gain under 0.1 us, which is what happened, but not by its cause. The slow one, by VectorE's bias addition, did not come in the changed kernel (1.22 us each time), but it did in e12 (4.13).

**Still open**: whether it is GpSimd's issue that holds TensorE up or the scatter's transfers behind it (in the chunk shown the first pause begins at 597.07, 0.17 us after the issue's end, the second at 598.70, within an issue), by what path, and why on the first chip, A and B but not on C and D. No run shows any of these. A variant that has e8's early start and keeps all issues off the attention with no one late behind it was not found; where e8 has pauses its chunk is no longer than where it has none (34.9 both), as the projection behind the attention waits for the difference.

## What to carry to other kernels

When a change shifts one engine's program against another's, compare the two in the middle as well as at the end: which instructions now stand beside which, above all long issues beside runs of very short matmuls. Read idle time that no semaphore explains ("issue") as a cost that can grow, and list it before predicting. An instruction that moves back takes everything behind it on the in-order engines along; here one independent step (rounding x) stood behind the moved one, and moving it ahead turned 0.9985 of before on chip B, in another set, into 0.979, while on chip D, without pauses, it won nothing (0.980 against 0.981). Try a pair of kernels on more than one chip before calling an order better.

## What the runs showed of the hardware

- TensorE's matmuls of 32x64 (one started every 15 ns) paused for 0.15 to 0.5 us at a time, up to four times in 128, while or just after GpSimd issued an indirect DMA; the same matmuls with a 1.3 us subtraction of GpSimd beside them did not (e5, e10).
- GpSimd's issue of a slot scatter took 0.96 us at its shortest and 1.78 with VectorE's addition of two 128x1024 tensors beside it, on a chip with pauses (e8) as on one without (c2).
- The first chip, A and B showed the pauses, C and D did not, with the same kernels. The same edit was worth 0.7%, 0.15% and 1.9% on the first chip, B and D. The kernel before took 1698 and 1708 us on C and D, and 1756 to 1777 us on the others (medians).
- VectorE's addition of two 128x1024 tensors took 1.22 us, 1.85 with 0.7 to 0.8 us of a GpSimd subtraction in it (c2) and 4.13 with two of them (e12).
- Writing a TensorE loop out, 122 blocks of program fetched instead of 21, moved a chunk by 0.1 us at most (e1: 0.9999 of the kernel before; the changed kernel is 0.9934 on the first chip and 0.9985 on chip B, and was not run beside e1).
- After a wait of 1.4 to 1.5 us ahead of the attention's projection TensorE was granted the 1.2 GHz level for some 3.4 us, in 19 of e12's 26 chunks.
- Eight reads of 64 KB in runs of 256 bytes kept SP's queue for 4.2 to 5.6 us in the changed kernel's loop, 4.84 in the median, against 7.1 to 9.7 us, 8.1 in the median, in runs of 64 bytes before (7.53 in [rows 6]). My estimate of 4.1 us from the Trainium skill's DMA: Bandwidth & Descriptors, section "Why small descriptors are slow (HBM only)", lies a little below all of them: the trace agrees in direction and rough size. In e7, where the same reads stand elsewhere against the other transfers, they took 5.3 to 7.2 us.
